# Moving 56 of 808 tiles of relation rows out of two short blocks into the block of matrix and layers

## The reference

```python
def reference(x, src, dst, edge_type_500, ...):
    edge_index = jnp.stack([src, dst])
    x = x + _L0_gnn_ref(_layernorm(x), edge_index, ...)      # 3 rounds of mean aggregation
    x = x + _L0_ffn_ref(_layernorm(x)[None], ...)[0]         # 16 experts, top 2
    x = x + _L1_gnn_ref(_layernorm(x), edge_index, edge_type_500, ...)
    x = x + _L1_ffn_ref(_layernorm(x)[None], ...)[0]         # 8 experts, top 2
    return x

def _L0_gnn_ref(x, ...):                                     # N = 3125, D = 256, 103125 edges
    h = x.at[0].set(mask_embed)
    deg = max(number of edges into each node, 1)
    for i in range(3):
        agg = segment_sum(h[src], dst) / deg
        z = agg @ Wl[i] + b[i] + h @ Wr[i]                   # then a folded batch norm, relu but for the last
        h = z + h
    return h

def _L1_gnn_ref(h, edge_index, edge_type, relation_emb, ...):
    r_uv = r_hc[edge_type]                                   # one row of 256 for each edge
    m = clifford_linear(h_src * r_uv, msg_w, msg_b)
    gate = jax.nn.sigmoid(r_uv.reshape(r_uv.shape[0], -1) @ gate_w.T + gate_b)
    m = m * gate[:, :, None] * norm[:, None, None]
    h_agg = segment_sum(m, dst)
    h_out = clifford_linear(h_hc + h_agg, upd_w, upd_b)
    return h_out
```

## Time and profile before

| what | us |
|---|---|
| median of 3 runs | 3947.94 |
| lowest and highest | 3929.95, 3977.62 |
| the profiled execution | 3907.93 |
| its span, first to last instruction | 3906.2 |

### The profile page before, as it was taken

The page is one execution under the profiler, slowest core; times in us unless marked ns, Lnnn a source line. Parts: engine busy times, 40 slices in busy tenths (PEclk is TensorE's granted clock), DMA queues, the critical chain, the costliest instruction groups (busy, mean ns, idle before and its releaser), DMA issues. The chain is left out here.

```text
span 3906.2 us, 54002 instructions
## 1 busy us (share of the span) xinstructions
PE 2592.3 (66%) x14033; PEld 1902.6 (49%) x14033; DVE 1511.1 (39%) x4513; ACT 1433.3 (37%) x3654; POOL 1956.1 (50%) x1945
## 2 busy tenths in 40 slices
PE   1567777688887885687603555555555555759997
PEld 1244545455655665566502333333333333559997
DVE  5566666531111003200163545444544554641110
ACT  0254554435542002232233333333333333435554
POOL 2535454454555551655436666666666666013332
PEclk9888888898988986899855667666766676879999
DMA  6644544455655553555526666566666665254332
GB/s 217 206 119 143 154 143 143 135 178 176 195 173 179 162 166 120 172 162 173 184 77 182 180 173 182 166 179 170 178 176 170 177 177 160 63 176 133 81 79 59
DMA packets 366599, 609.48 MB, mean 156 GB/s; under 512 B 82339, under 2 KB 231980, under 8 KB 363537
## 3 DMA queue, kind: packets, MB, share of 16 engines
q1 hardware_dynamic: 261984, 334.64, 26.8%
q0 software_dynamic: 100208, 265.56, 25.3%
q10 hardware_dynamic: 4144, 6.20, 0.4%
HBM read 443.45 MB, written 167.60 MB: 156 GB/s over the span
## 5 line engine op out<-in xcount | busy, mean ns | idle before, releaser
L656 POOL DMA_INDIRECT agg_r_rows<-h_table,parts_and_x x832 | 842.8, 1013 | 482.9 <-issue 216.5
L709 PE MATMUL agg_r_sums<-agg_r_rows,agg_r_onehot 128*128 128x257 f32 x1664 | 670.0, 544 | 577.2 <-issue 243.7
L1408 POOL DMA_INDIRECT rl_buf<-r_table,kinds x632 | 630.1, 997 | 648.2 <-DMA relation_rows<-rl_buf 456.8
L709 PEld LDWEIGHTS agg_r_sums<-agg_r_rows,agg_r_onehot 128*128 128x128 f32 x1664 | 399.8, 265 | 836.8 <-issue 520.1
L682 DVE TENSOR_TENSOR acc<-acc,agg_r_sums 128x257 f32 (+1 forms) x836 | 353.6, 423 | 629.6 <-issue 458.8
L623 ACT ACTIVATE agg_r_gap<-iota,parts_and_x 128x128 f32<-128x128 f32 x832 | 287.0, 392 | 634.7 <-PE agg_r_sums L709 362.9
L1806 PE MATMUL f_pH<-f_xT,f_w 128*128 128x128 f32 x2816 | 352.2, 283 | 45.0 <-DMA f_w<-in_L_ffn_w 18.7
L1806 PEld LDWEIGHTS f_pH<-f_xT,f_w 128*128 128x128 f32 x2816 | 336.9, 196 | 78.4 <-issue 42.8
L1176 PE MATMUL ly_acc<-matrix_and_parts 128*128 128x256 bf16 x1250 | 358.2, 287 | 24.6 <-issue 23.9
L1175 PE MATMUL ly_acc<-matrix_and_parts 128*128 128x256 bf16 x1250 | 356.8, 285 | 23.0 <-issue 22.6
L1174 PE MATMUL ly_acc<-matrix_and_parts 128*128 128x257 bf16 (+1 forms) x1250 | 356.7, 285 | 17.7 <-issue 17.1
(11 more groups left out here) (394 smaller groups left out, 3518.3 us busy)
## 6 DMA issues: line engine op xcount, KB each, us to landing
agg_r_rel<-relation_rows SPq DMA_DIRECT2D x404, 260.0 KB
relation_rows<-rl_buf SPq DMA_DIRECT2D x316, 260.0 KB
relation_rows<-f_rr_buf POOLq DMA_DIRECT2D x60, 260.0 KB
f_w<-in_L_ffn_W SPq DMA_DIRECT2D x28, 512.0 KB, 5.1
f_w<-in_L_ffn_W SPq DMA_DIRECT2D x14, 1024.0 KB
agg_r_rows<-h_table,parts_and_x POOLq DMA_INDIRECT x832
ly_zin<-zh SPq DMA_DIRECT2D x50, 256.0 KB
zh<-ly_out SPq DMA_DIRECT2D x50, 256.0 KB
```

Of the source, the lines that this page charges most:

```text
L656: pool.indirect_dma_start(rows[:, n % SLOTS, t, :], None, table, bass.IndirectOffsetOnAxis(ap=indices[:, t:t + 1], axis=0)).then_inc(s_row ...
L709: last = nc.tensor.matmul(sums[:, (2 * n + t) % BANKS, 0:used], onehot[:, n % HOT, t, :], rows[:, n % SLOTS, t, 0:used], start=True, stop= ...
L1408: pool.indirect_dma_start(self.buf[:, n, g, :], None, self.table, bass.IndirectOffsetOnAxis(ap=self.c.kinds[:, at:at + 1], axis=0)).then_i ...
```

## The change

`SHARES` goes from (16, 40, 632, 120) to (688, 120). The two `RelationRows` beside `edge_blocks` and the dense product are gone with their buffers and their five cleared semaphores each, with the gathers on POOL and the stores on ACT and SP; POOL has no work of its own left in those two blocks. `matrix_and_layers` prepares tiles 0 to 687. Its loops are unchanged.

```diff
--- before.py
+++ after.py
@@ -69,7 +69,7 @@
 NTP = NT
 MW = NT * P
 
-SHARES = (16, 40, 632, 120)
+SHARES = (688, 120)
 assert sum(SHARES) == EDGE_TILES
 GW = 3 * D + 2
 TURN, DENSE = 9, 14
@@ -425,7 +425,7 @@
                 pool.wait_ge(s_copy, 16)
 
 
-def edge_blocks(nc, c, loads, relation):
+def edge_blocks(nc, c, loads):
 
 
 
@@ -453,17 +453,7 @@
         s_tot, s_c, s_cum, s_u, s_groups, s_tables = (k.sem(f"gt_{x}") for x in ("tot", "c", "cum", "u", "groups", "tables"))
         s_lists, s_link, s_row, s_near, s_turn, s_spread, s_out, s_saved, s_more, s_pick = (k.sem(f"eb_{x}") for x in (
             "lists", "link", "row", "near", "turn", "spread", "out", "saved", "more", "pick"))
-        work = RelationRows(nc, c, k, "re", *relation)
         with nc.Block() as block:
-
-            @block.gpsimd
-            def _(pool):
-                work.fetch(pool, 0, work.pairs)
-
-            @block.scalar
-            def _(act):
-                work.store(act, 0, work.pairs)
-                work.stored(act)
 
             @block.sync
             def _(sp):
@@ -898,11 +888,11 @@
         return out
 
 
-def gnn0_start(nc, c, I, x_dram, room, g, z, folded, relations):
+def gnn0_start(nc, c, I, x_dram, room, g, z, folded):
 
     with Core(nc) as k:
         f, h = Fold(c, room), c.x
-        edge_blocks(nc, c, f.loads(c, I, x_dram), relations[0])
+        edge_blocks(nc, c, f.loads(c, I, x_dram))
         stats = k.sb("ln0_stats", [P, NT, 6])
         mean, var, tmp = (k.sb(f"ln0_{x}", [P, NT]) for x in ("mean", "var", "tmp"))
         hT = k.sb("d0_hT", [P, 2, KD, P])
@@ -911,7 +901,6 @@
         s_link, s_var, s_root, s_bn, s_bnroot, s_w, s_norm, s_turn, s_hT, s_z, s_hi, s_rest, s_q1, s_q2, s_z0, s_saved = (
             k.sem(f"d0_{x}") for x in ("link", "var", "root", "bn", "bnroot", "w", "norm", "turn", "hT", "z", "hi", "rest", "q1",
                                        "q2", "z0", "saved"))
-        work = RelationRows(nc, c, k, "r0", *relations[1])
         with nc.Block() as block:
 
             @block.vector
@@ -1008,7 +997,6 @@
 
             @block.sync
             def _(sp):
-                work.store(sp, 0, 8)
                 sp.wait_ge(s_norm, NT)
                 sp.dma_start(z[:, D:2 * D].rearrange("(t p) d -> p t d", p=P), h[:, :, :]).then_inc(s_saved, 16)
                 sp.wait_ge(s_w, 4)
@@ -1016,17 +1004,10 @@
                     sp.dma_start(folded[l - 1, :, 0:4 * D], f.w[:, l, :, :].rearrange("p k n -> p (k n)")).then_inc(s_saved, 16)
                     sp.dma_start(folded[l - 1, :, 4 * D:5 * D], f.shift[:, l, :]).then_inc(s_saved, 16)
                 for b in range(NJ):
-                    work.store(sp, 8 + 2 * b, 10 + 2 * b)
                     sp.wait_ge(s_z0, (b + 1) * J)
                     sp.dma_start(z[b * J * P:(b + 1) * J * P, 0:D].rearrange("(t p) d -> p t d", p=P), f.z[:, b * J:(b + 1) * J, :])\
                         .then_inc(s_saved, 16)
                 sp.wait_ge(s_saved, 16 * (5 + NJ))
-                work.store(sp, 8 + 2 * NJ, work.pairs)
-                work.stored(sp)
-
-            @block.gpsimd
-            def _(pool):
-                work.fetch(pool, 0, work.pairs)
 
 
 def matrix_and_layers(nc, c, records, m, ga, gb, x1, zh, folded, x_dram, relation):
@@ -1448,8 +1429,8 @@
             for name, (shape, dt) in tables.items():
                 c.tab[name] = kk.sb(name + "_work", shape, dt)
             prepare_edges(nc, c, I, edges, c.records, r_table, relation_rows, room)
-            gnn0_start(nc, c, I, I["x"], flat, g, zh[0], folded, [relation(0), relation(1)])
-        matrix_and_layers(nc, c, c.records, m, g, gb, c.x, zh, folded, I["x"], relation(2))
+            gnn0_start(nc, c, I, I["x"], flat, g, zh[0], folded)
+        matrix_and_layers(nc, c, c.records, m, g, gb, c.x, zh, folded, I["x"], relation(0))
     return x1, h_tables, zh[0]
 
 
@@ -2456,7 +2437,7 @@
 
         experts(nc, c, I, "f0", E0, F0, TILES0, False, I["L0_ffn_w1"], I["L0_ffn_b1"], I["L0_ffn_w2"], I["L0_ffn_b2"],
                 logits[0], xn_table, None, ACT.Relu, finish0,
-                (r_table, relation_rows, sum(SHARES[:3]), SHARES[3]))
+                (r_table, relation_rows, SHARES[0], SHARES[1]))
         gnn1(nc, c, I, relation_rows, h1_table, logits[1], xn_table)
 
         experts(nc, c, I, "f1", E1, F1, TILES1, True, I["L1_ffn_W1"], I["L1_ffn_b1"], I["L1_ffn_W2"], I["L1_ffn_b2"],
```

## The result

| what | before | changed |
|---|---|---|
| median, us | 3942.24 | 3979.80 |
| lowest, highest | 3923.56, 3977.62 | 3952.67, 4019.46 |
| the profiled execution, its span | 3907.93, 3906.2 | 3972.12, 3970.4 |

A forecast was written before the change was run, and what follows sets the result against it. The prediction took no single bound: each block ends with its latest engine, POOL's gathers pacing the tail. +53.2 - 1.4 - 1.0 - 2.7 - 0.5 = +47.6 us on the median 3947.94 gives 3995.5 us; range 3965 to 4030.

The forecast's parts named there:

- What bounds the end of the block, and the count of pairs: End of `matrix_and_layers`: 27 pairs left behind the loop, paced by POOL at 2.54 us a pair.
- slow gathers: Rival: the tail's pairs take 3.13 us each, or stores and gathers collide; +61.4 us, 4009 us; chance 0.12.
- covered: Rival: spare pairs get done before DVE's end at 1489.2, leaving only the gains; -5.6 us, 3942 us; chance 0.06.
- Node tiles are not delayed: End of `matrix_and_layers`: the last node tile's loads stand ahead of the 30 stores in SP's stream, so no delay.
- the prediction's signs: Expected in the changed profile, among others: TensorE, DVE and ACT idle about 53 us before the gate's first instruction.
- The early gains: `edge_blocks` and the dense block, freed of relation rows, get shorter: 1.4, 1.0, 2.7 and 0.5 us.
- a sign of being wrong: The prediction is wrong if, among other signs, the two short blocks shrink by more than 10 us together.
- the end of `edge_blocks`: Without ACT's stores SP ends the block, 1.4 us gained; shorter waits for lists and table, 1.0 us.
- the last stores: End of the dense block: SP done at 182.0, not 184.7, without the last two relation stores; 2.7 us gained.
- The other stores of this block stood between `zh` pieces that wait for DVE, so their leaving moves nothing: Dense block: removing relation stores other than the last two gains nothing.
- The clock doesn't pay back: Against a rival: TensorE's 53 us rest lets the experts run nearer full clock; +24 us, 3972 us; chance 0.07.
- the main term: Tail of `matrix_and_layers`: the block ends 53.2 us later, on SP's last store behind POOL's gathers; bounds +51 to +67.

The follow-up runs named there:

- e9: The changed kernel itself, unaltered, run once more on a slower chip: 3991.30 us against 3941.00 for the kernel before, ratio 1.0144.
- e12: Changed kernel with gathers from pair 320 on taking 16 rows, not 128, stores whole; slower chip, once: 4034.70 us beside 4008.43 for the kernel before.
- e2: Kernel before, short blocks keeping their tiles, with the block of matrix and layers preparing all 688: 3990.29 us, ratio 1.0148.
- e7: Changed kernel with four pairs a node tile in the last loop, not three; faster chip: 3352.61 us against 3309.77 for the kernel before, ratio 1.0133.
- e11: Changed kernel with the tail's 27 stores issued after the last node tile; slower chip, once: 4050.52 us beside 4008.43 for the kernel before.
- e6: Changed kernel with gathers from pair 320 on taking 16 rows, not 128, stores whole; faster chip, once: 3345.60 us beside 3309.77 for the kernel before.
- e5: Changed kernel with the tail's 27 stores issued after the last node tile; faster chip, once: 3379.48 us beside 3309.77 for the kernel before.

## Why the prediction was right, and where it wasn't

**What bounds the end of the block, and the count of pairs:** right. 27 pairs are left, SP's stream has one group of 30 stores, and they are gathered at 1.26 us a gather, without a gap over 0.31 us. From the first of the last 54 gathers to the last it is 66.8 us (1453.71 to 1520.54), 2.52 us a pair against 2.54 taken. The rivals "slow gathers" (3.13 us a pair) and "covered" are both refuted by this row. No gather of the tail took 7.95 us as that of the earlier trace rows did, and the longest of all 688 is 2965 ns. By the Trainium skill (SBUF — State Buffer, "SBUF: two separate sides"), GpSimd can't write its descriptors while VectorE runs an instruction in a mode that holds their shared ports; VectorE had two instructions at the start of these 54 gathers (1454.6 and 1455.1) and none from there to the last one, and the trace agrees.

**"Node tiles are not delayed":** this is the step that failed. The prediction argued from SP's stream, where the last tile's loads stand ahead of the 30 stores, and took TensorE and DVE to end before POOL. The loads were in time; TensorE's instructions were not, and neither was the release of DVE behind them. The sum that was added 8.2 us behind the one before it came 75.1 us behind it here, and the last one 8.1 us later. So the block ends on DVE at 1538.9 and not on SP's last store, landed at 1525.7. From the last load, the term came to 66.4: 54.7 for POOL's pairs, which is the 53.2, and 11.7 that SP waited for TensorE (in e9 56.9, of which 3.0). TensorE and DVE didn't idle for some 53 us ahead of the gate, as the prediction's signs had it, but ended last. What ties TensorE and DVE to POOL's gathers stays open. The clue was in the trace of before, in the page's groups that this prediction didn't use: the layers' matmuls sat idle for "issue" there too.

```profile
L1176 PE MATMUL ly_acc<-matrix_and_parts 128*128 128x256 bf16 x1250 | 358.2, 287 | 24.6 <-issue 23.9
```

**The early gains:** right in sign, half in size: 12.4 us for 5.6. The prediction had named more than 10 us here as a sign of being wrong, and by that sign this part is. Measured 4.0 us at the end of `edge_blocks` (forecast 1.4 + 1.0), 2.9 for the last stores (forecast 2.7), 0.6 for the clearings (0.5), and 4.9 on TensorE in the dense block, for which the prediction had nothing. Its sentence "The other stores of this block stood between `zh` pieces that wait for DVE, so their leaving moves nothing" looked at the stores and left the gathers out; the lost idle time for "issue" lies beside them. The Trainium skill (DMA: Bandwidth & Descriptors, "Issuing engines are not separate DMA queues") holds that transfers of all queues interleave on the same engines. The shorter waits for lists and table, 0.8 and 1.0 us less, agree with it. Whether the 4.9 us are a matter of transfers wasn't tried: e12 shows it for the tail alone.

**The clock doesn't pay back:** right; the gate's first window (1545 to 1550) is at 0.50 as in the earlier trace rows, and the stretch behind it got no shorter.

**The sum:** +47.6 against a measured +44 (37 to 51). By the gate it is +49.5: the tail's 66.4, less 12.4 in the short blocks, less 4.6 in the stretch from the first load to the last, which varies by 46 us between two traces of the same kernel (1278.9 here, 1325.3 in e9; 1283.5 before, 1306.2 in e2). So the mechanism of the main term is right, and that the sum comes so near is in part luck: the tail cost 13 us more than its term, the short blocks gave 7 more, and the rest lies inside the scatter of that stretch. Both errors are argued to have one cause, gathers beside TensorE; if so, a change that only added such gathers would have met it twice with the same sign.

## What to carry to other kernels

Where work is passed out in small shares beside other loops, count the seats first: a pair too many costs its producer's full period (2.52 us here), and a share per step that exceeds the step (four pairs of 2.54 beside a tile of 8.06) costs what it exceeds it by (1.9 us a tile in e7). Before calling a stream of GpSimd gathers hidden behind TensorE, look for TensorE's idle time ended by "issue" where the gathers run without a gap; if it is there, the gathers may cost TensorE time even though no semaphore ties them together. Compare also the last matmul of a sum with the instruction that waits for it: here 0.31 us was the rule at undisturbed tiles, and 31.7 and 62.4 us were the second sign. A program should be measured on more than one chip before such a cost is called a property of the kernel.

## What the runs showed of the hardware that was not expected

- While POOL issues indirect DMAs without a gap, TensorE comes down to one instruction in 1.40 us on the slower chips (e2, e9, e11, e12 and the first trace), whether a gather moves 128 rows or 16 and whether stores run or not. In the first trace it is back to 25 matmuls in 5 us from 1529.6 on, 8.1 us behind the last gather's end. How the two engines are tied is not settled: the traces show no wait between them, and no late block of instructions.
- DVE's instruction that waits for a sum's last matmul starts 0.31 us behind it in the last four tiles of the trace of before and the last twelve of e6, and 62.4 us behind it in the tail of the first trace (31.7 in e9).
- On one chip such kernels have no such pause: idle time for "issue" ahead of `ly_acc`'s matmuls is 0.0 us in e5 (36.8 and 39.1 us for two of the groups in the changed kernel), and the kernel before takes 3310 us there against 3940. What differs between the chips wasn't found; the executions on them also lie minutes apart.
- Not settled either: the changed kernel itself was not timed on the faster chip. e6, run once, is 35.8 us above the kernel before there; with whole gathers 5.8 us more, +42, a ratio near 1.013, again worked out.
